# Zero-padded copies of y in blocks of four rows with runs of four columns, in place of halves of rows with pairs of columns

## The reference, cut to what matters

```python
# block 1, on y = layernorm of x over j
q, k, v = (einsum('oc,ncij->noij', w, y) for w in (Wq, Wk, Wv))
qk  = einsum('ncij,nchj->nihj', q, k) / d
qrq = einsum('ncij,chi->nihj', q, rq) / d
krk = einsum('ncij,chi->nihj', k, rk) / d
weight = softmax(qk + Gq * qrq + Gk * krk, axis=3)
out = einsum('nihj,nchj->ncij', weight, Gv1 * v) + einsum('nihj,chi->ncij', weight, Gv2 * rv)
x = x + out
# block 2, on the tokens (c, i) of x, layernormed over j: W, a batch norm over all tokens,
# then y_t = sigmoid(wx_t + y_(t-1) @ V.T) along the 1024 tokens of an image, and a residual
```

## Time and profile before

| what | us |
|---|---|
| median of the 3 runs shown | 137.07 |
| lowest and highest of them | 134.37, 137.10 |
| the profiled execution, device time | 134.09 |
| its span | 132.3 |

### The profile page before, as it was taken

One profiled execution on the slowest core, in us unless ns is written; L12 is line 12 of the kernel. 1 busy time (PEld: TensorE's weight loads), 2 busy tenths in 40 slices (PEclk: granted clock), 3 DMA queues, 4 the chain that ended last, 5 costly groups with the idle time before them and its releaser, 6 DMA issues.

```text
span 132.3 us, 4756 instructions
## 1 busy us (share of the span) xinstructions
PE 101.9 (77%) x2078; PEld 74.9 (57%) x2080; DVE 95.3 (72%) x151; ACT 79.4 (60%) x162; POOL 67.9 (51%) x77
## 2 busy tenths in 40 slices
PE   0694997799779999887995996756959969999000
PEld 0331232169779999775994995421312449999000
DVE  5898928857210396897790595799999597889991
ACT  7967874970913546598892512442652699999100
POOL 8996863994000057528700998998960000008840
PEclk9999999999999999999999999999999999999975
DMA  3892651084000000060061000000000000002666
GB/s 147 249 319 23 152 126 40 0 202 128 0 5 5 5 7 5 9 143 19 5 136 27 5 5 5 5 0 0 0 0 0 0 0 0 5 2 58 198 178 201
DMA packets 7968, 7.98 MB, mean 60 GB/s; under 512 B 2124, under 2 KB 6220, under 8 KB 7948
## 3 DMA queue, kind: packets, MB, share of 16 engines
q1 hardware_dynamic: 7948, 7.69, 22.0%
HBM read 2.97 MB, written 2.10 MB: 38 GB/s over the span
## 4 chain that ended last, share of the span: by engine, by line
PE 25%; POOL 22%; DVE 22%; ACT 13%; issue 7%; DMA 6%; SPq 2%; POOLq 0%; ACTq 0%; DVEq 0%
POOL y_tile L437 6%; ACT warm L680 5%; PE ps L1036 5%; PE ps L1072 4%; POOL u_tile L431 4%; DVE xin L356 4%; POOL y_tile L443 4%; PE ps L1051 4%; PE ps L1084 3%; DVE y_tile L362 3%; PE ps L1028 3%; POOL y_tile L196 3%; DMA spread_parts<-rel_tile 3%; PE ps L1060 3%; DMA xin<-in_x_dram 3%
## 5 line engine op out<-in xcount | busy, mean ns | idle before, releaser
L412 POOL TENSOR_TENSOR att_tile<-att_tile,soft 128x1024 f32<-128x1024 f32 x4 | 7.8, 1955 | 20.6 <-DVE soft L784 20.6
L362 POOL TENSOR_TENSOR y_tile<-xin,u_tile 128x256 f32<-128x256 f32 (+1 forms) x7 | 7.1, 1045 | 20.8 <-DVE xin L356 20.8
L1036 PE MATMUL ps<-spread_parts,u_tile 128*32 128x64 f32 x512 | 12.9, 252 | 2.0 <-issue 2.0
L1036 PEld LDWEIGHTS ps<-spread_parts,u_tile 128*32 128x32 f32 x512 | 12.2, 190 | 2.4 <-issue 2.4
L933 DVE TENSOR_SCALAR ps<-att_tile,bnv 128x512 f32<-128x512 f32 x15 | 11.0, 807 | 1.6 <-ACT warm L680 1.6
L1072 PE MATMUL ps<-spread_parts,rv_t 128*32 128x128 f32 x256 | 11.2, 339 | 0.9 <-DMA spread_parts<-rel_tile 0.9
L1084 PE MATMUL ps<-spread_parts,v_tile 128*32 128x64 f32 x512 | 9.0, 222 | 3.3 <-issue 3.2
L1095 PE MATMUL ps<-rel_tile,w_bd 128*128 128x512 f32 x16 | 8.7, 623 | 3.2 <-DVE rel_tile L848 2.5
L1072 PEld LDWEIGHTS ps<-spread_parts,rv_t 128*32 128x32 f32 x256 | 10.3, 119 | 1.4 <-issue 1.1
L1148 PE MATMUL ps<-blank 128*128 128x512 bf16 x40 | 9.8, 379 | 1.5 <-DVE u_tile L826 1.3
L778 DVE TENSOR_TENSOR att_tile<-ps,rel_tile 128x1024 f32<-128x1024 f32 x4 | 4.9, 1214 | 8.4 <-ACT rel_tile L513 8.4
(11 more groups left out here) (112 smaller groups left out, 242.2 us busy)
## 6 DMA issues: line engine op xcount, KB each, us to landing
out_dram<-y_tile SPq DMA_DIRECT2D x8, 256.0 KB, 2.3
xin<-in_x_dram SPq DMA_DIRECT2D x3, 512.0 KB, 4.6
spread_parts<-att_tile SPq DMA_DIRECT2D x8, 128.0 KB, 2.4
spread_parts<-rel_tile SPq DMA_DIRECT2D x8, 128.0 KB, 2.8
xin<-in_x_dram SPq DMA_DIRECT2D x2, 256.0 KB, 2.8
spread_parts<-u_tile SPq DMA_DIRECT2D x4, 128.0 KB, 2.3
att_tile<-in_L_conv_rv_dram SPq DMA_DIRECT2D x4, 128.0 KB, 3.0
att_tile<-in_L_conv_rq_dram SPq DMA_DIRECT2D x1, 128.0 KB, 6.1
```

The costliest lines, as they stand in the source:

```text
L362: return eng.tensor_tensor(result[:, :, rows, :], back[:, at:at + P * k].rearrange("p (q i j) -> p q i j", q=Q, i=k), x2[:, :, rows, :], A ...
L1036: return nc.tensor.matmul(ps[group(q), first + j // 8, at:at + G * HALF].rearrange("p (g i) -> p g i", g=G), u[:, q, :, j], y_bd[:, q, :, ...
```

## The change

y_bd gets the order (b=8, jq=8, i=4, t=4): a block b of four rows, then fours of columns, then the four rows, then the four columns. All who write and read it follow. In memory:

- the moving operand of a score matmul was 16 elements 8 bytes apart for each image; it becomes four stretches of 4 elements 16 bytes apart, the stretches 512 bytes apart;
- the moving operand of a relative score matmul was 16 pairs, 128 bytes from pair to pair, for each image; it becomes 8 fours, 64 bytes from four to four;
- the copies write 4 adjacent elements with 64 bytes from four to four, where they wrote pairs 128 bytes apart. Their source is y in its own order as before.

The instructions on each engine, their order, sizes, waits and outputs stay as they are. att_bd keeps its pairs, so L1072 and L1084 don't change. The first 512 elements of a piece are rows 0 to 15 in both orders.

```diff
+RUN_Y = 4
-        y_bd = spread4[:, :, :, :].rearrange("p q g (b jp i t) -> p q g b jp i t", b=2, i=HALF, t=RUN)
+        y_bd = spread4[:, :, :, :].rearrange("p q g (b jq i t) -> p q g b jq i t", b=PIECES4, i=ROWS, t=RUN_Y)
...
-        def in_pairs(t):
-            return t.rearrange("p (b jp i t) -> p b i jp t", b=2, i=HALF, t=RUN)
+        def in_fours(t, b):
+            return t.rearrange("p (b jq i t) -> p b i jq t", b=PIECES4, i=ROWS, t=RUN_Y)[:, blocks(b)]
+
+        def blocks(b):
+            return slice(PIECES4 // 2 * b, PIECES4 // 2 * (b + 1))
+
+        def by_fours(t):
+            return t.rearrange("p (b i) (jq t) -> p b i jq t", i=ROWS, t=RUN_Y)
...
-            return in_pairs(spread4[group(g), q, g, :])[:, b]
+            return in_fours(spread4[group(g), q, g, :], b)
...
-            return by_pairs(y[group(g), q, HALF * b:HALF * (b + 1), :])
+            return by_fours(y[group(g), q, HALF * b:HALF * (b + 1), :])
...
-                    nc.scalar.copy(in_pairs(turned_y[q])[:, b], by_pairs(y[:, q, HALF * b:HALF * (b + 1), :])).then_inc(S["y_turned_act"], 1)
+                    nc.scalar.copy(in_fours(turned_y[q], b), by_fours(y[:, q, HALF * b:HALF * (b + 1), :])).then_inc(S["y_turned_act"], 1)
...
-                return nc.tensor.matmul(ps[group(q), first + j // 8, at:at + G * HALF].rearrange("p (g i) -> p g i", g=G),
-                                        u[:, q, :, j], y_bd[:, q, :, half, j // RUN, :, j % RUN],
+                return nc.tensor.matmul(ps[group(q), first + j // 8, at:at + G * HALF].rearrange("p (g b i) -> p g b i", g=G, i=ROWS),
+                                        u[:, q, :, j], y_bd[:, q, :, blocks(half), j // RUN_Y, :, j % RUN_Y],
...
-                        ins = nc.tensor.matmul(side_bank(n)[group(q), P * k:P * (k + 1)].rearrange("p (g jp t) -> p g jp t", g=G, t=RUN),
-                                               r_fac[:, ROWS * n + k, :], y_bd[:, q, :, n // 4, :, ROWS * (n % 4) + k, :],
+                        ins = nc.tensor.matmul(side_bank(n)[group(q), P * k:P * (k + 1)].rearrange("p (g jq t) -> p g jq t", g=G, t=RUN_Y),
+                                               r_fac[:, ROWS * n + k, :], y_bd[:, q, :, n, :, k, :],
```

## The result

| | before, median us (runs) | changed, median us (runs) | ratio changed / before, 95% interval |
|---|---|---|---|
| first comparison | 134.65 (4 of 7) | 133.08 (7 of 7) | 0.9885 [0.9845, 0.9925] |
| second, another chip | 133.73 (17 of 29) | 133.92 (9 of 12) | 1.0001 [0.9961, 1.0040] |
| third, another chip | 133.49 (18 of 29) | 133.47 (9 of 12) | 0.9963 [0.9917, 1.0009] |

The ratio and its interval are estimated from the runs themselves and are not the quotient of the two medians.

The account below looks back on a forecast made before the run. TensorE was taken to bound the chain to relative piece 3, then softmax and DMA. TensorE's own path, 1.3 - 0.8 + 3.8 - 0.5 less 0.9 slack, gave +2.9 us: 135.7 + 2.9 = 138.6 us, range 133.9 to 142.3.

Parts of the forecast that it names:

- The bound and the paths: TensorE bounds the chain to relative piece 3, then softmax and DMA; TensorE has its own path beside the softmax.
- the prediction's sum: Chain to piece 3: +2.5 - 1.2 = +1.3 us; TensorE's own path: 1.3 - 0.8 + 3.8 - 0.5 - 0.9 = +2.9.
- The price of a single element: Scores: 64 elements 16 bytes apart take 159 ns a round; half 0 +2.5 us, half 1 +3.8 us.
- the supply of instructions: TensorE's instructions come in blocks of 256, one per 3.7 us at fastest, so no round gains below 117 ns.
- the slack: Before L1072: TensorE's own path ends 0.91 us before the DMA on which L1072 waits.
- the stride is nearly free: Rival on scores: the moving operand takes up to 117 ns a round; 1.2 us gain, 134.5 us; chance 0.26.
- the forecast's lower end: Bottom of the forecast's +1 to +4.3 us, for score rounds between about 140 and 170 ns; forecast's chance 0.42.
- The relative scores: L1051 reading fours falls from 150 to 117 ns a round: pieces 0 to 3 -1.2 us, 4 to 7 -0.8.
- The sign "with gaps": In the profile after, L1051 was to run at 29 ns a record with "issue" gaps.
- The copies: Copies of y writing fours: at best -0.04 us each on ScalarE; taken as 0.
- The range: Whole kernel: 133.9 us (134.37 - 0.5) to 142.3 us (137.07 + 5.2, the dearer single element).
- its second case: The rival that the stride is nearly free: scores at up to 117 ns a round, 1.2 us gain, chance 0.26.

Follow-up runs that it names:

- whole rows: Changed kernel with y_bd in runs of 32 columns, so scores read single elements 128 bytes apart: 143.78 us beside 135.92, single runs.
- near weights: Scores' stationary operand read as 32 adjacent elements, single runs: changed kernel 132.92 us, kernel before 135.14, beside 135.92.
- relative scores alone: Kernel before with only the relative scores reading fours 64 bytes apart: 133.85 and 132.49 us beside a median of 133.73.
- pairs in blocks of four rows: Changed kernel with runs of two columns in place of four: 132.79 us beside 133.73 (ratio 0.993), then 133.34 beside 133.49 (0.995).

## Why the prediction was wrong, step by step

**The bound and the paths: held.** The chain runs over TensorE to the end of piece 3, and then over the softmax and the DMA. The arithmetic of the two paths can be tried on whole rows. At 197 ns a round a half is 12.6 us; the prediction's sum then says chain +5.0 - 1.2 = +3.8, TensorE 3.8 - 0.8 + 6.2 - 0.5 - 0.9 = +7.8 us. Measured: 7.2 in the profiles by the stretch from L1068 (28.82) to L1080 (68.67), 39.9 us against 32.7. The two single runs differ by 7.9, but the profile of whole rows also has the granted clock at 0.50 from 98 to 104 us, so they say less. The paths were right; which of the two ends last was not, and that follows from the next step.

**The price of a single element: the step that failed.** The prediction said "each element may now be a hop of its own", and "I take the mean of L1051 and L1072, 159 ns, as the nearest case of 64 hops in a moving operand". The changed scores run at 120, 30 ns a record and not the 35 to 45 that were to be its sign. The +2.5 us that this put on half 0 measured +0.2 (7.6 to 7.8), since the supply of instructions had held half 0 at about 117 ns a round before; the +3.8 us on half 1 measured about +1.5 (6.4 to 7.9), and the slack, the faster pieces 4 to 7 and the smaller gap took them up. With 120 for 159 the prediction's own sum gives -1.1 us for the chain and -1.8 for TensorE: the DMA releases L1080, as the profile shows, and the kernel gains about 1.1 us where the forecast was a loss of 2.9. The rows used for the price, L1051, L1072, the weight loads and L573, all have 128 bytes between their pieces, and the change has 16. I took the number of pieces as what costs; the runs show that the step matters as much: 64 single elements cost 120 to 124 ns at 16 and 32 bytes and 197 at 128. For a step of 128 bytes the prediction's 150 to 176 would even have been too little.

The rival "the stride is nearly free" had the sum, at up to 117 ns a gain of 1.2 us, and the profiled span came down by 1.2. It had half the reason. The stride isn't free: with near weights the step from 8 to 16 bytes takes a round from 60 to 116 ns. What hid it was that the new price lies next to the 117 ns of the supply, which is the rival's upper bound. That was luck: no row of the kernel before told 120 from 150.

The sum at 150 ns in that rival, +2.1 us, is also a slip: by the prediction's own terms it is 0.8 - 0.8 + 3.2 - 0.5 - 0.9 = +1.8, and the forecast's lower end, at 140 ns, is +0.6 and not +1. Neither changes the verdict.

**The relative scores: held.** 117 expected, 114 measured; 4.93 us expected to fall to 3.7, measured 3.60. The sign "with gaps" didn't come: no "issue" row stands in L1059. The scattered pairs were the limit and the matmul's other operand was not, since with the relative scores alone the same fall shows. The rule of the Trainium skill ("SBUF — State Buffer", Specifications (TRN2)), two hits a 16-byte line for full bandwidth, is borne out on its other side: with near weights one hit a line, at 16 bytes a step, costs 116 ns against 60 for two. But a pair is not enough when the pairs lie 128 bytes apart (150 against 118 at 32 bytes), and one hit a line has no single price (120 and 197). Why L1072, the same kind as L1051 at the same granted clock of 1.00, takes 168 ns and not 150 stays open.

**The supply of instructions: held.** Slower scores filled the gaps, so half 0 went from 7.6 to 7.8 us although its matmuls became a third slower; faster ones only lengthened the gaps, twice. This is why the 120 ns cost nothing on the chain. The gap in the second L1060 was expected to vanish at 159 ns; at 120 it fell from 0.54 to 0.25, and the second and third profiles of the change have no such row.

**The copies: held, to 0.03 us.** 614 ns in place of 640. The first two together, the ones near the chain, take 1.14 us in place of 1.17; VectorE's six take 2.90 in both.

**The size in whole runs: less than the sum, and open.** The stretch from the start of L1060 or L1068 to the end of the last weighing on VectorE before L778 or L786 (L801 or L809, two instructions) holds both groups of matmuls that the change touches on the chain. In the profile before it takes 56.23 - 28.11 = 28.1 us. In that of the change the last weighing is

```profile
53.81 1.32 DVE L809 TENSOR_TENSOR rel_tile<-att_tile,soft 128x512 f32<-128x512 f32 x2
```

and the stretch takes 55.13 - 28.19 = 26.9; it takes 26.8 and 27.1 in the second and third profiles. So 1.0 to 1.3 us are won there each time. Around this stretch are waits that differ as much from one execution to the next: the first DMA of x takes 3.67 us on the chain before and 3.79, 4.37 and 3.97 in the three profiles of the change; from the end of L801 or L809 to L1072 or L1080, over the DMA of the weights, 4.5 us before and 4.4, 4.0 and 4.9 after; the gap in weighted_sums of half 0 1.61 before and 1.41, 1.35 and 2.06 after.

Behind it the granted clock differs too. The pages of before and of the change, in the same 40 slices:

```profile
PEclk9999999999999999999999999999999999999975
PEclk9999999999999999999999999996899999999985
```

In the profile of the change it falls to 0.50 between 89 and 93 us, in its third one between 91 and 95, in the second and in that of before not until the end. From the start of the first matmul of L1095 or L1103 to the end of the last, 16.4 us pass before and in the second profile, 17.1 in the first and third. Over the fourteen profiles of this case the same stretch takes 15.7 to 16.8 us where the granted clock doesn't fall in it, and 17.1 to 18.6 where it does, whatever the order of y_bd. So in the first and third profiles some 0.7 us go with the clock, in matmuls that the change doesn't touch. Whether the change has a part in these waits and falls, or whether the differences between the three comparisons are their scatter, isn't settled.

**The range.** Its low end, 133.9, took 0.5 us off the fastest run shown, although its second case had 1.2 to give and the profiled execution was lower still. And the middle, 138.6, stood on a mean of 135.7 for the kernel before, from four runs at two levels; the medians above have it at 133.5 to 134.7. Of the 5.5 us between 138.6 and 133.1 about 1 is this level; the rest is a loss of 2.9 forecast where a gain of 1.6 was measured.

## What to carry to other kernels

Price a scattered operand by a row with the same step and the same run, not only the same number of pieces: here single elements nearly doubled in cost between 8 and 16 bytes and rose by some 60% between 32 and 128, while 32 runs of four cost no more than adjacent elements at either distance tried. Where two groups of matmuls read one buffer in crossing orders, look for an order in which both keep pairs close together, as with pairs in blocks of four rows. And before a faster matmul is counted, look for "issue" gaps at even distances: behind them the time belongs to the supply of instructions. And before a difference of a microsecond is put down to a change, look at the granted clock of both profiles, slice by slice.

## What the runs showed of the hardware that I had not expected

- A matmul's moving operand of 64 fp32 elements, four column groups in parallel: 60 ns a round at 8 bytes a step, 116 to 124 at 16 and 32, 197 at 128. Of 128 elements in pairs: 115 to 122 ns 32 bytes apart, 150 to 168 at 128. In fours: 111 to 117 at 64 bytes, 112 at 256.
- A stationary operand of 32 fp32 elements 128 bytes apart holds a round of four at 88 ns where 32 adjacent ones let it run at 60.
- Fast matmuls get 256 instructions (128 matmuls with their weight loads) in 3.45 to 4.0 us, from gap to gap. In the kernel before with near weights the matmuls of such a block took 2.1 us and the gaps before and after them 1.6 and 1.9. The next 16 KB packet of instructions starts 1.1 to 1.3 us after a block has begun, and TensorE goes on 2.2 to 2.9 us after it starts.
- With the granted clock at 0.50 for over half of the stretch, relative_values with pairs 32 bytes apart took 5.5 us; at 1.00 it took 3.9.
